# Unread TensorE products in the first five iterations of a state-space scan, where later iterations issue the output's products

## What is computed

```python
xr, gate = jnp.split(x @ W_in.T, 2, axis=-1)
# xr -> + t_emb, convolution over time, silu, norm -> xn; Bm, Cm, dt from xn
def step(h, inputs):
    ad, bd, xt, ct = inputs
    h = jnp.clip(h * ad[:, :, None] + bd[:, :, None] * xt[:, None, :], -10.0, 10.0)
    yt = jnp.einsum('bd,bdh->bh', ct, h)
    return (h, yt)
_, ys = jax.lax.scan(step, h0, (Ad, Bd, xn, Cm))
y = ys.transpose(1, 0, 2) + D * xn
return y * jax.nn.silu(gate) @ W_out.T
```

## Time and profile before

| | us |
|---|---|
| median of 3 runs | 3006.66 (3006.36 to 3008.82) |
| the profiled execution, its own time | 3012.6 |
| its span, from the first to the last instruction | 3010.8 |
| around the span (3012.6 less 3010.8) | 1.8 |
| scan: first B·x product to last h | 475.5 to 1487.5 of the span |
| TensorE busy over the span | 2809.3 (93%) |
| VectorE busy over the span | 2131.5 (71%) |
| mean granted TensorE clock | 0.956 |

### The profile page before, as it was taken

How to read it: one execution, slowest core, us unless ns; L and a number is a source line. 1 busy time by engine, 2 the same in 40 slices (tenths; PEclk the granted TensorE clock), 3 DMA queues, 4 the chain that set the end, 5 groups by cost and what they waited for, 6 DMA issues and landing times. The chain is left out here.

```text
span 3010.8 us, 53576 instructions
## 1 busy us (share of the span) xinstructions
PE 2809.3 (93%) x19705; PEld 1319.2 (44%) x19706; DVE 2131.5 (71%) x3145; ACT 1114.4 (37%) x1913; POOL 1057.5 (35%) x432
## 2 busy tenths in 40 slices
PE   7999845889999999999879999969999999999999
PEld 3444322445555555555436677643333333333334
DVE  3789865889999999999754344256677777677624
ACT  2677741111111111111121221116666666666620
POOL 0000001134434344443312011006667777777730
PEclk9999957789999999999989999979999999999999
DMA  3245484466666666666543344354324344343364
GB/s 102 99 171 177 171 252 105 104 141 165 157 161 162 167 153 160 162 158 161 161 143 131 135 151 145 126 168 104 98 70 129 95 121 110 93 127 106 96 198 169
DMA packets 246894, 421.93 MB, mean 140 GB/s; under 512 B 45848, under 2 KB 114072, under 8 KB 240360
## 3 DMA queue, kind: packets, MB, share of 16 engines
q1 hardware_dynamic: 164056, 329.92, 36.8%
q10 hardware_dynamic: 82704, 90.32, 12.9%
HBM read 258.88 MB, written 160.98 MB: 139 GB/s over the span
## 5 line engine op out<-in xcount | busy, mean ns | idle before, releaser
L871 DVE CUSTOM_DVE_ANT_0 b_h<-b_h,b_bx,b_bounds_all 128x256 f32<-128x256 f32 x2048 | 947.6, 535 | 68.6 <-PE b_bx L975 55.1
L1503 DVE TENSOR_REDUCE e_half_max<-ef_banks 128x4 f32<-128x2048 f32 x256 | 585.9, 2292 | 233.2 <-PE ef_banks L1456 233.2
L1646 POOL TENSOR_TENSOR e_pair_sum<-e_probs 128x2048 f32<-128x2048 f32 x128 | 585.7, 4576 | 264.5 <-PE ef_banks L1495 215.3
L1615 ACT ACTIVATE e_probs<-ef_banks 128x512 f32<-128x512 f32 x1024 | 555.8, 595 | 309.4 <-PE ef_banks L1470 307.6
L959 POOL TENSOR_TENSOR b_b_weights<-b_bd_all,b_mask_b 128x512 fp32r<-128x512 f32 x64 | 81.2, 1269 | 909.1 <-issue 472.7
L1470 PE MATMUL ef_banks<-e_qs,e_ks 97*128 97x512 f32 x1024 | 381.9, 452 | 3.9 <-DVE e_half_max L1503 3.6
L1028 ACT COPY b_y_stage<-b_y_psum 128x128 f32<-128x128 f32 x256 | 67.9, 265 | 743.7 <-PE b_y_psum L985 739.7
L975 PE MATMUL b_bx<-b_x_moving,b_b_weights 24*128 24x512 f32 x1024 | 262.1, 507 | 62.6 <-POOL b_c_weights L961 39.5
L1470 PEld LDWEIGHTS ef_banks<-e_qs,e_ks 97*128 97x128 f32 x1024 | 154.5, 188 | 331.4 <-ACT e_probs L1615 312.9
L985 PE MATMUL b_y_psum<-b_h,b_c_weights 128*32 128x128 f32 x8224 | 283.8, 280 | 1.8 <-ACT b_y_stage L1028 1.3
L1480 PE MATMUL ef_banks<-e_probs,e_v 128*32 128x512 f32 x2048 | 273.6, 606 | 0.4 <-ACT e_probs L1615 0.4
(11 more groups left out here) (186 smaller groups left out, 2985.8 us busy)
## 6 DMA issues: line engine op xcount, KB each, us to landing
b_x_moving<-xn_parts SPq DMA_DIRECT2D x248, 128.0 KB
e_ks<-qk_parts ACTq DMA_DIRECT2D x42, 512.0 KB, 4.7
e_qs<-qk_parts ACTq DMA_DIRECT2D x84, 256.0 KB, 3.5
xn_full<-a_xn SPq DMA_DIRECT2D x32, 512.0 KB, 3.3
xn_parts<-a_hi SPq DMA_DIRECT2D x64, 256.0 KB, 2.5
xn_parts<-a_lo SPq DMA_DIRECT2D x64, 256.0 KB, 2.5
silu_gate<-b_sg ACTq DMA_DIRECT2D x64, 256.0 KB, 5.9
scan_out<-b_y_stage ACTq DMA_DIRECT2D x256, 64.0 KB, 4.3
```

The costliest lines, as they stand in the source:

```text
L871: return nc.vector._custom_dve(bass.dve_ops.TENSOR_ADD_SAT, **operands)
L1503: nc.vector.tensor_reduce(out=half_max[:, u // UNITS % 2, :, r // NH, r % NH], in_=(banks[:, u % 2 * GROUP:(u % 2 + 1) * GROUP] if u < FIR ...
L1615: nc.scalar.activation(probs[:, g % 4, h, :], p_exp[h % 2], ACT.Exp).then_inc(exps, 1)
L1646: nc.gpsimd.tensor_tensor(out=pair_sum[:, t % 2], in0=probs[:, (2 * t) % 4], in1=probs[:, (2 * t + 1) % 4], op=ALU.add).then_inc(paired, 1)
```

## The change

In `piece_of` an output piece for which there is no tile yet issues one product instead of none. It has the shape and type of a real output piece: 128 columns of `w_gate` as the stationary operand, 512 columns of `w_gate` as the moving operand, float32, into `p_out`, as a group of its own. It waits for nothing and signals nothing. Nobody reads it.

```diff
@@ -914,6 +914,9 @@
                 mm = nc.tensor.matmul(p_out[:], yg_t[:, m, :], w_out[:, m, :], start=(m == 0), stop=(m == NM - 1))
                 if m == NM - 1:
                     mm.then_inc(out_ready, 1)
+            else:
+                _, m = piece
+                nc.tensor.matmul(p_out[:], w_gate[:, m % NK, 0:P], w_gate[:, m % NK, HALF:2 * HALF], start=True, stop=True)
```

## The result

| | before | after |
|---|---|---|
| median (6 runs each, same chip) | 3008.22 (3006.36 to 3012.20) | 2994.03 (2990.92 to 2995.34) |
| ratio, 95% interval | | 0.995, 0.9937 to 0.9962 |
| profiled execution, its own time | 3012.6 | 2995.34 |
| its span | 3010.8 | 2993.6 |
| first h to last h | 476.4 to 1487.5 | 476.4 to 1468.4 |

The forecast was 2987.6, with a range of 2984 to 2992.5: the right sign, 6.4 us too low, and outside the range. The gain is 14.2 us where 19.0 was forecast.

What follows compares the result with a forecast made beforehand. Early scan rounds were taken as bound by TensorE at half clock, then VectorE; later ones by TensorE. Savings of 1.76, 15.4 and 1.91 us made 19.0, so 3006.66 - 19.0 = 2987.6 us, range 2984 to 2992.5.

Steps and rivals of the forecast that it cites:

- that the pieces hold the clock: Early scan iterations: with the added products the clock stays at 1.00 from before 482.44; ten slow stretches go.
- the round of 3.783 us: Early scan iterations: each round with added products takes 3.783 us, as in later iterations; four make 15.13 a half.
- the scan's part of the sum: Scan from 482.44 to 653.35: savings of 1.76, 15.4 and 1.91 us, together 19.0.
- The slower rival: Early scan halves: the clock falls all the same, added products cost 0.8 us a half, 3014.6 us; chance 0.04.
- Most of that lies in the scan: Profile page's low slices, 376 to 677 us: claimed to lie mostly in the scan, which starts at 475.5.
- The three signs of being wrong: Between 490 and 650: a 0.50 clock row, a round over 0.1 us off 3.78, a DMA wait over 1 us.
- After the scan nothing is changed: Stages behind the scan: unchanged in length, all moving up by the same 19 us.
- Rival 5: Behind the scan: half the gain or more given back by a transfer or slow stretches elsewhere, 2997 to 3007; chance 0.03.
- That leaves some 0.9 us; no wait, and a wait less than before.: B·x loads in early iterations: needed after 11.35 us, tightest took 10.35, so no wait.
- Rival 2: Early scan: smaller gain, rounds over 3.783 us or a wait for second-iteration loads, 2989 to 2992; chance 0.12.
- 3006.66: Whole kernel: median of the runs shown before the change, from which 19.0 us was taken.
- The rule of the Trainium skill: Scan's ten slow stretches: half of each 6.70 us returned, some 33.5 us, 2973.2; weighed as a rival, chance 0.01.

Runs made afterwards that it cites:

- two_iterations: The change with unread products in the first two iterations only, none in the third to fifth; 3003.97 us, ratio 0.9982 against the kernel before.
- warm_start: The change plus 16 more unread products ahead of the scan; 2995.89 us, ratio 0.9958.
- after_c: The change, unaltered, in a third profile; 992.8 us from first to last h, 1523.7 us from last h to end.
- width_384: The change with unread products of 384 columns instead of 512; 2988.73 us, ratio 0.9940.
- half_width: The change with unread products of 256 columns instead of 512; 2995.56 us, ratio 0.9961.
- first_round: The change with unread products only in rounds 3 and 7, none in rounds 4 and 8; 2996.59 us, ratio 0.9960.

## Why the prediction was wrong, point by point

**Right.** The reading of what bound the first five iterations; that the pieces hold the clock; the round of 3.783 us (3.78 measured); halves of 15.13 (15.12) and 15.52 (15.52); the first slow round left as it was; the scan's part of the sum, 19.0 (19.1 in the first profile, 18.2 on the mean of four). `two_iterations` shows the effect half by half. The slower rival, that the clock falls all the same, did not happen in any half of the four profiles of the change.

One reading was loose. "Most of that lies in the scan" holds for the time from 376 to 677, not for the low clock: the granted clock is 0.57 over the 99 us ahead of the scan and 0.82 over the 202 us in it, some 85 and 73 us at half clock. The sum does not use it.

The three signs of being wrong that the prediction ends with all lay inside the scan, so they could not show what went wrong behind it. In the first profile only one appears, by a hair: the round from 505.03 to 508.94 takes 3.91 us.

**Wrong, first step: "After the scan nothing is changed ... it all moves up by the same 19 us."** The part behind the scan is made of the same instructions, but its length depends on where the clock falls in it, 1523.4 us before and 1525.0 after, mean of three and of four. That term is +1.6 and not 0. That it is a fixed cost of the change is not shown: variants of it took 1520.3 to 1527.7. Rival 5 named the mechanism (slow stretches that fall elsewhere), but priced it at half the gain or more, which did not happen; a loss of a few us had no term in the sum, only some room in the range, though the page's own clock row showed falls there.

**Wrong, second step: "That leaves some 0.9 us; no wait, and a wait less than before."** The wait that I looked at, in the second half of the second iteration, did go. The load before it, for the iteration's first half, stands behind `bd_all`'s transfers. It was needed at 509.17 in the kernel before and at 508.38 in the change, from the same start at 475.55, and lands about then. I took "needed three rounds later: 11.35 us in the new timing" for all loads and never asked what was ahead of it in its queue. It costs 0.8 us on average in the change, and 3 to 5 us of waiting, with a fall of the clock behind it, as soon as anything else makes the first iteration shorter. Rival 2 named the place and priced it once at 1 to 3 us.

**Wrong, third: the level and the width.** I took 3006.66, the median of three runs, for the kernel's time, and their spread of 2.5 us for its scatter. The runs beside the experiments have medians of 3009.07 to 3011.22. In the comparison that counts, 3008.22, it is 1.6 of the 6.4 us, the other 4.8 being 19.0 less 14.2; it is no step of the argument. A range around one profiled sum should have held the scatter ahead of the scan and behind it, 5 and 7 us over all the profiles.

By the terms: -18.2 + 1.6 + 0.3 is -16.3 for the profiles; the medians say -14.2. The last 2 us lie in which executions were profiled: the three of the kernel before took 3010.4 us on average, 2.2 above its median of 3008.22, and the four of the change 2994.0, just its median. Seven profiles of parts that vary by 3 to 5 us settle no more than that.

The rule of the Trainium skill that I weighed (TensorE: Matmul & The Clock Gate, "HAM oscillation — how this bites in real kernels") puts the loss at half of the throttled time. For these ten stretches that is an estimate of 33.5 us; measured are 19. VectorE's pace and the added products take the rest, as argued from the rows.

## What to carry to other kernels

Where a stage's clock alternates, look for what TensorE leaves out compared with a stage where it does not, and price the whole round at the full clock, not the slow stretch. Unread work can be made just wide enough to stay under the next bound: with 384 columns the halves were mostly 14.3 to 14.6 us (one of 14.95), with 512 they were 15.1. With half of the work the clock fell again in two to four halves, and no kernel with narrower products was clear of the change by its interval. A transfer that arrives just in time before a speed-up is the next wait: check what is queued ahead of it.

## What the runs showed of the hardware that was not expected

- A wait of 3.3 to 5 us at full clock is followed by gate pieces at half clock, wholly or in part (505.17 and 505.89 in `warm_start`), while behind the 0.84 us of `after_c` they took 1.98 us, the full clock's time. With the fall the half is longer by more than the wait: 22.3 against 15.1 us there for 4.97 of waiting, 19.5 against 14.3 in `width_384` for 3.32.
- The same 1523 us of instructions behind the scan took 1520.3 to 1527.7 us, with no change there. The difference is TensorE's busy time (1441.9 to 1449.1 us), not its waits.
- A half iteration with too little TensorE work has two lengths, 14.05 to 14.6 us and 16 to 20, in one and the same execution (`half_width`, `first_round`). So a half with less work was faster or slower than the change's 15.12 us, and their mean no better.
